# Attention with early loads for the feed-forward: x loaded and normalized rows stored as four transfers of 256 KB or as one of 1 MB

## The reference

```python
scale, shift = split(silu(sin_emb(timestep)) @ W_ada + b_ada)      # per batch
x = ln(src) * (1.0 + scale) + shift                                # src: 16 x 512 x 512
q, k, v = x @ Wq + bq, x @ Wk + bk, x @ Wv + bv                    # 16 heads of 32
scores = q @ k.T / sqrt(32) + attention_bias                       # 16 x 16 x 512 x 512
probs = softmax(where(src_mask, -inf, scores))
x = x + (probs @ v) @ Wo + bo
h = ln(x) * g2 + beta2
ff = gelu2(h @ W1 + b1) @ W2 + b2                                  # gelu2(x) = x * sigmoid(1.702 x)
out = rotate(x + ff, theta, phi)                                   # groups of 4 columns, per batch
```

## Time and profile before

| | |
|---|---|
| median of three runs | 3260.62 us |
| profiled execution | 3258.98 us, its span 3257.2 us |
| TensorE matmuls | 3155.3 us busy, 97% of the span |
| TensorE weight loads | 2377.1 us, 73% |
| VectorE | 2147.9 us, 66% |
| GpSimd | 2017.4 us, 62% |
| ScalarE | 1862.8 us, 57% |
| DMA packets | 785.15 MB, mean 241 GB/s, 79.2% of 16 engines on SyncE's queue |
| loads of x | 16 of 1024 KB, median 7.2 us from issue to landing |
| stores of normalized rows | 16 of 1024 KB, median 7.9 us |

### The profile page before, as it was taken

The page is one execution under the profiler, slowest core; times in us unless marked ns, Lnnn a source line. Parts: engine busy times, 40 slices in busy tenths (PEclk is TensorE's granted clock), DMA queues, the critical chain, the costliest instruction groups (busy, mean ns, idle before and its releaser), DMA issues.

```text
span 3257.2 us, 52385 instructions
## 1 busy us (share of the span) xinstructions
PE 3155.3 (97%) x16592; PEld 2377.1 (73%) x16592; DVE 2147.9 (66%) x4446; ACT 1862.8 (57%) x4057; POOL 2017.4 (62%) x1246
## 2 busy tenths in 40 slices
PE   6999999999999999999979999999999999999998
PEld 4777777777777777777647687787877868687787
DVE  4777787777787777877768655544645455464542
ACT  3777777777777777777754343443424334253443
POOL 3888888888888888889648633434333443434413
PEclk9999999999999999999989999999999999999999
DMA  6999999898999998999857686675867757586665
GB/s 204 272 273 268 261 276 269 266 266 269 257 281 271 266 265 260 279 273 264 261 177 249 230 261 206 203 254 175 262 201 236 234 179 251 180 262 205 200 203 172
DMA packets 440432, 785.15 MB, mean 241 GB/s; under 512 B 57024, under 2 KB 106176, under 8 KB 440160
## 3 DMA queue, kind: packets, MB, share of 16 engines
q1 hardware_dynamic: 440160, 781.82, 79.2%
HBM read 591.76 MB, written 89.19 MB: 209 GB/s over the span
## 4 chain that ended last, share of the span: by engine, by line
PE 45%; POOL 2%; DVE 1%; ACT 1%; issue 1%; ACTq 0%; DVEq 0%; POOLq 0%
PE ps_out L1449 21%; PE ps_first L1429 16%; PE ps_first L1470 6%; PE ps_first L1482 1%; POOL g_lo L1690 0%; PE ps_out L1470 0%; DVE w_ring L1815 0%; POOL w_ring L1708 0%; ACT g_hi L1548 0%; DVE tmp L1930 0%; DVE g_later L1809 0%; POOL y_rows L1744 0%; DVE y_sum L1849 0%; DVE g_now L1809 0%; DVE h_lo L1880 0%
## 5 line engine op out<-in xcount | busy, mean ns | idle before, releaser
L718 POOL TENSOR_TENSOR bias_ring<-bias_ring,maskb 128x1024 f32<-128x1024 f32 x512 | 1092.9, 2148 | 235.3 <-DMA bias_ring<-in_fside_Bx16xSxS_dram 232.8
L1449 PE MATMUL ps_out<-w_ring,g_hi 128*128 128x512 f32 x2048 | 677.9, 398 | 15.2 <-POOL w_ring L1708 7.1
L1429 PE MATMUL ps_first<-h_hi,w_ring 128*128 128x512 f32 x1792 | 554.5, 391 | 5.9 <-issue 5.7
L1690 POOL TENSOR_TENSOR g_lo<-g_now,g_hi 128x512 fp32r<-128x512 f32 x128 | 169.6, 1325 | 608.9 <-ACT g_hi L1548 608.9
L823 PE MATMUL ps_score<-k_rows,q_rows 96*128 96x512 f32 x1024 | 493.2, 482 | 0.3 <-DVE negmax L961 0.3
L1449 PEld LDWEIGHTS ps_out<-w_ring,g_hi 128*128 128x128 f32 x2048 | 385.3, 188 | 110.1 <-issue 31.0
L874 ACT ACTIVATE probT<-ps_probT 128x512 f32<-128x512 f32 x512 | 305.3, 596 | 261.5 <-PE ps_probT L836 167.9
L961 DVE CUSTOM_DVE_ANT_0 prob_last<-ps_score,bias_ring 128x512 f32<-128x512 f32 x512 | 348.9, 686 | 145.4 <-PE ps_score L823 131.9
L961 DVE CUSTOM_DVE_ANT_0 prob_first<-ps_score,bias_ring 128x512 f32<-128x512 f32 x512 | 349.1, 684 | 124.1 <-PE ps_score L823 111.5
L836 PE MATMUL ps_probT<-ident,prob_first 128*128 128x128 f32 x2048 | 393.4, 273 | 25.5 <-ACT probT L874 19.9
L1449 PE MATMUL ps_out<-w_ring,g_lo 128*128 128x512 f32 x1024 | 399.4, 390 | 0.0
(11 more groups left out here) (182 smaller groups left out, 5624.3 us busy)
## 6 DMA issues: line engine op xcount, KB each, us to landing
bias_ring<-in_fside_Bx16xSxS_dram SPq DMA_DIRECT2D x512, 512.0 KB, 5.9
w_ring<-w_parts SPq DMA_DIRECT2D x240, 512.0 KB, 3.8
w_ring<-w_parts SPq DMA_DIRECT2D x392, 256.0 KB, 3.5
k_rows<-k_hi SPq DMA_DIRECT2D x512, 64.0 KB, 5.1
q_rows<-q_hi SPq DMA_DIRECT2D x512, 64.0 KB, 3.7
x_wo<-in_x_dram SPq DMA_DIRECT2D x16, 1024.0 KB, 7.2
normal_rows<-x_wo SPq DMA_DIRECT2D x16, 1024.0 KB, 7.9
k_rows<-k_lo SPq DMA_DIRECT2D x256, 64.0 KB, 4.5
```

What stands on the lines that cost most here:

```text
L718: pool.tensor_tensor(tile, tile, maskb[:, 2 * half:2 * half + 2, :], ALU.add).then_inc(masked.sem, 1)
L1429: mm = pe.matmul(ps[:, BANK[n], :], w1r[:, place, w, cols], h[:, n, c, :], start=(c == 0 and k == 0 and not onto), stop=(c == 1 and k == 2 ...
L1449: mm = pe.matmul(ps_out[:, t, :], a[:, k % 2, cols], w2r[:, k % VR, w, :], start=(m == 0 and n == 0), stop=(m == NF - 1 and n == 2))
L1690: pool.tensor_tensor(GLO[:, k % 2, :], src, GHI[:, k % 2, :].bitcast(F32), ALU.subtract).then_inc(glo_done.sem, 1)
```

## The change

Each transfer of 1 MB of x, and each store of the normalized rows, becomes four of 256 KB (128 rows of one tile, 2 KB each). The counters `x_in` and `normal_out` count 64 where they counted 16, so a wait still is for all of x. In a batch the stores stand at slots 22, 23, 24 and 26 where one stood at 24, the loads at 36, 38, 40 and 41 where one stood at 36, and the mask at 45 where it stood at 44. Each store waits for its own tile to be normalized; the waits ahead of the load stand before its first tile. The slots of the statistics stay.

```diff
-                load_x(sp, 0)
+                for t in range(4):
+                    load_x(sp, 0, t)
...
-    x_in = Tally(sem("x_in"), 1, 16)
+    x_in = Tally(sem("x_in"), 1, 16 * NT)
...
-    def load_x(sp, b):
-        sp.dma_start(xn[:, :, :], x[bass.ds(b, 1), :, :].rearrange("o (t p) d -> p (o t) d", p=P)).then_inc(x_in.sem, 16)
+    def load_x(sp, b, t):
+        sp.dma_start(xn[:, t, :], x[bass.ds(b, 1), t * P:(t + 1) * P, :].rearrange("o p d -> p (o d)")).then_inc(x_in.sem, 16)
...
-    normal_out = Tally(sem("normal_out"), 1, 16)
+    normal_out = Tally(sem("normal_out"), 1, 16 * NT)
...
-    STORE_AT, LOAD_AT, MASK_AT = 24, 36, 44
+    STORE_AT, LOAD_AT, MASK_AT = (22, 23, 24, 26), (36, 38, 40, 41), 45
...
-                    if slot == STORE_AT and mode in AHEAD:
-                        normed.wait(sp, b, NT - 1)
-                        sp.dma_start(normal_dram[bass.ds(b + 1, 1), :, :].rearrange("o (t p) d -> p (o t) d", p=P),
-                                     xn[:, :, :]).then_inc(normal_out.sem, 16)
-                    if slot == LOAD_AT and b + 2 < B:
-                        xt_done.wait(sp, b, NC - 1)
-                        normal_out.wait(sp, b, 0)
-                        load_x(sp, b + 2)
-                    if slot == LOAD_AT and mode == LAST:
+                    if slot in STORE_AT and mode in AHEAD:
+                        t = STORE_AT.index(slot)
+                        normed.wait(sp, b, t)
+                        sp.dma_start(normal_dram[bass.ds(b + 1, 1), t * P:(t + 1) * P, :].rearrange("o p d -> p (o d)"),
+                                     xn[:, t, :]).then_inc(normal_out.sem, 16)
+                    if slot in LOAD_AT and b + 2 < B:
+                        t = LOAD_AT.index(slot)
+                        if t == 0:
+                            xt_done.wait(sp, b, NC - 1)
+                            normal_out.wait(sp, b, 0)
+                        load_x(sp, b + 2, t)
+                    if slot == LOAD_AT[0] and mode == LAST:
```

## The result

The changed kernel takes 3347.38 us (median of 4 runs, 3343.1 to 3351.48) against 3260.63 us before in the same comparison: 1.0268 times the time, 95% interval 1.0249 to 1.0287, 87 us more. 3330 was forecast, in a range of 3294 to 3354. The profiled execution has a span of 3344.0 us.

What follows compares the result with a forecast made beforehand. TensorE, busy 97% of the span, was taken as the bound, so its idle decides. The profiled 3258.98 us plus 66 for 14 batches, 3 for startup and 1.6 from profiled run to median gave 3330 us, range 3294 to 3354.

Steps and rivals of the forecast that it cites:

- What the wait is: Middle batches, slot 43: VectorE's first statistics wait for all four x tiles and stand 6.3 us for the fourth.
- When it lands: Fourth x tile, middle batches: lands behind 3.2 MB in the saturated queue, 14.7 us after the first x issue.
- C: Rival, wait at slot 43: last x tile lands as on a quieter queue, in 3.3 us; 3265 to 3268 us, chance 0.08.
- D: Rival, middle batches: q_lo lands sooner and the statistics find their data, only relief is seen; 3248 us, chance 0.04.
- VectorE's and TensorE's idle: Middle batches: VectorE stands 6.3 us for x, TensorE idles 5.3 us for VectorE's copy queued behind the statistics.
- The clock: TensorE behind each 5.3 us idle: runs at the 1.2 GHz level for a while, costing 1.6 us a batch.
- The sum: Middle batch: 0.81 of idle plus clock is 5.6 us, less the old 0.87, net 4.7; 66 us over 14 batches.
- the 0.81 for what is recovered later: Middle batches: share of a batch's loss that stays, 3.85 of 4.78 us, since later small waits shrink.
- rival B: TensorE after 5 us idle: clock stays low twice as long, 3.2 us a batch; 3348 us, chance 0.15.
- Startup: Before attention: three more issues per x load or store delay q and k rows and mask; 3 us, bounds 0 and 5.4.
- Stores and mask: Middle batches: three more store issues hidden by SyncE's waits for VectorE, mask one slot later; 0, stores at most 1.8 us.
- The relief for q rows: Middle batches: with 512 KB less ahead, q_lo lands about 2 us sooner; ScalarE's q_hi wait nearly gone, by itself removing 19.5 us.

Runs made afterwards that it cites:

- e4: Changed kernel, same transfers, but the first statistics wait for the first x tile alone and the second ones for the other three: 3243.68 us, ratio 0.9947.
- e1: Changed kernel with x loaded again in one 1 MB transfer at slot 36, stores still cut and mask still later: 3256.33 us, ratio 0.9992.
- e2: Changed kernel with the normalized rows stored again in one 1 MB transfer at slot 24, x still cut: 3348.83 us, ratio 1.0266.
- e6: Changed kernel with the four x loads at slots 36, 37, 38, 39 and one wait for all at slot 43: 3286.00 us, ratio 1.0084.
- e5: Changed kernel with 16 more unused matmuls on TensorE ahead of its wait at slot 45 in the fourteen batches: 3323.16 us, ratio 1.0200.
- e7: Kernel of e4 with x loaded in one transfer in the setup and the pass before batch 0: 3239.82 us, ratio 0.9941.
- e8: Kernel before the change, x whole but issued at slot 40, statistics at slots 50, 53, 56, 59: 3247.60 us, ratio 0.9968.
- e3: Changed kernel with all four x loads issued one behind the other at slot 36: 3269.11 us, ratio 1.0024.

## Why the prediction was right

*What the wait is.* Right, and shown by e4: with every transfer in its place, only the wait changed, and the loss was gone. e1 and e2 leave no other part of the change with a share in it.

*When SyncE issues the fourth tile.* Forecast 7.9 us after the first, 8.1 in the worked batch, 8.0 on average (7.4 to 8.7).

*When it lands.* Forecast 14.7 us after the first issue, from the bytes in the queue; 15.2 measured, with the statistics beginning at 15.3. e6 moved 0.8 MB behind the tile, and the landing came 3.1 us sooner, as those bytes say. The rivals fall with this: C, since the last tile took 7.2 us and not 3.3, and D, since the statistics waited fourteen times. The rule of the Trainium skill that stood beside C (page "DMA: Bandwidth & Descriptors", section "Anatomy of one DMA — SWDGE (gpsimd) path"), about 2 us and the bytes at 436 GB/s, gives an estimate of 2.6 us for 256 KB. The trace does not agree behind a full queue, where the fourth tile took 5.4 to 9.8 us. It agrees for the tile issued at 53.79 us, in the pass before batch 0, where no bias tiles are on the queue:

```profile
DMA to landing us min/median/max: 2.6/2.6/2.6
```

*VectorE's and TensorE's idle.* Forecast 6.3 and 5.3 us a batch, measured 7.0 and 5.9. Most of the difference is the later landing; VectorE also asks 0.1 us sooner, at 8.2.

*The clock.* The prediction counted 1.6 us a batch, as behind the 3.18 us idle of before. The traces give 1.9, since 4.3 us at half speed lie behind each idle where 3.4 lay behind that one. So this term was sized too small, but by little. Of the 85 us that the expectation of e5 speaks of, 26 lie within the idle and cost nothing.

*The sum.* Forecast 4.7 us a batch net, measured 105.32 - 99.04 = 6.3, and this is the weakest part. The sizes (0.6 of idle, 0.3 of clock) explain some 0.7 of the missing 1.6. The larger part is the 0.81 for what is recovered later, with the old cost of 0.87 that came from the same pair of intervals. New idle and clock are 5.9 + 1.9 = 7.8 us a batch, old ones 1.4 + 0.2, and the difference of 6.2 is close to the 6.3 that the kernel lost, so next to nothing was recovered. e5 says the same of the clock alone. Why the one pair of intervals kept only 0.81 is open.

*The number.* 3347 lies in the range, 17 us above the forecast and on the 3348 of rival B. That is chance: B's reason, 3.2 us of clock a batch, is not what the traces show (1.9).

*Startup.* Forecast 3, measured 2.4 up to the first load of batch 0; e7 takes it back.

*Stores and mask.* Forecast 0. (The last tile is normalized at 688.61 + 2.07 = 690.7, not 690.8, which changes nothing.) e1, which has both, lies between 6.5 us below and 1.3 us above the kernel before, and e2 gets nothing back.

*The relief for q rows.* Here I was too hopeful: ScalarE's wait was to be nearly gone and is 24.9 us of 43.8. Half of x is still ahead of the last q row. It cost nothing that the trace shows, since VectorE's wait lies over it: TensorE has no wait for ScalarE's copy left. In e4, where VectorE's wait is gone, the waits for q rows are shorter than before on average, and this goes with the gain over the kernel before; e8, which cures the same wait another way, gains too.

## What to carry to other kernels

When a transfer is cut in pieces and spread, ask for the time of the last piece, and cut its wait as well: the same four transfers cost 87 us with one wait for all and saved 15 us with two waits. On a full queue a transfer lands, on average, when the bytes ahead of it are through (1 MB at 6.7 us in e3, 2.4 MB at 12.2 in e6, 3.2 MB at 15.2 in the changed kernel), so count those up to it, where it stands in the issue order, and compare with the instruction that needs it. And an idle of TensorE of some 5 us must be priced with the slower clock behind it, here 1.9 us for 5.9 of idle, and hardly anything of either came back later.

## What the runs showed of the hardware that was not expected

With idles of TensorE of 3.8 to 7.9 us, the granted clock was at half speed for 6.1 us a batch on average. In twelve of the fourteen batches it fell before the idle had ended, so the part that costs time, 4.3 us a batch, is less than the clock's record alone suggests. 16 unused matmuls inside the wait took 22 to 24 us off the kernel.

The last x tile of the changed kernel took 5.4 us to land in one batch and 9.8 in another with the same issue order. Four of the five longest are among the first five batches. What makes the queue slower there is open, and so is the like spread in e6.
